# The order of a node tile's closing work in the edge loop of a graph attention layer

## The reference

```python
hh = (x @ W).reshape(n, H, D)                       # 8 heads of 32
scores = leaky_relu(s_src[src] + s_dst[dst], 0.2)
e = jnp.exp(scores - m[dst])                        # m: segment max
alpha = e / segment_sum(e, dst)[dst]
out = segment_sum(hh[src] * alpha[:, :, None], dst) + x
out = elu(layernorm(out) * gamma + beta)
x = x + out
gate_logits = layernorm(x) @ gate_w + gate_b        # then top 2 of 16 experts
```

## Time and profile before

| | us |
|---|---|
| median of three runs | 3359.18 (3358.12 to 3366.66) |
| the profiled execution, its own time | 3364.55 |
| its span in the profile | 3362.8 |

### The profile page before, as it was taken

One profiled execution on the slowest core, in us unless ns is written; L12 is line 12 of the kernel. 1 busy time (PEld: TensorE's weight loads), 2 busy tenths in 40 slices (PEclk: granted clock), 3 DMA queues, 4 the chain that ended last, 5 costly groups with the idle time before them and its releaser, 6 DMA issues. The chain is left out here.

```text
span 3362.8 us, 43456 instructions
## 1 busy us (share of the span) xinstructions
PE 1790.6 (53%) x9190; PEld 1462.5 (43%) x9191; DVE 1683.8 (50%) x3940; ACT 1018.8 (30%) x2031; POOL 1840.0 (55%) x1936
## 2 busy tenths in 40 slices
PE   6243544445454454544535444454544535999975
PEld 5132433334343343433434333343433435898964
DVE  6554545545455464554645445454554542333346
ACT  4232323233232332323233232332323312333442
POOL 2455656566565666656566565665656523555520
PEclk9676777777677776777767777776777767999987
DMA  5443434434343343433434344343443436333343
GB/s 185 114 116 98 122 103 125 116 106 119 105 123 116 107 119 105 123 110 115 117 105 123 102 125 117 107 119 103 124 118 106 119 82 205 101 103 101 106 142 130
DMA packets 184424, 393.55 MB, mean 117 GB/s; under 512 B 52129, under 2 KB 106810, under 8 KB 178116
## 3 DMA queue, kind: packets, MB, share of 16 engines
q0 software_dynamic: 92288, 267.12, 27.9%
q1 hardware_dynamic: 75876, 111.73, 10.7%
q10 hardware_dynamic: 16224, 14.30, 1.5%
HBM read 356.52 MB, written 36.47 MB: 117 GB/s over the span
## 5 line engine op out<-in xcount | busy, mean ns | idle before, releaser
L1265 POOL DMA_INDIRECT gat<-table,idx x1632 | 1547.0, 948 | 999.0 <-issue 452.5
L1362 PE MATMUL ps_sum<-msg,hot 128*128 128x264 f32 x3332 | 1076.1, 493 | 1049.3 <-DVE msg L1409 779.1
L1362 PEld LDWEIGHTS ps_sum<-msg,hot 128*128 128x128 f32 x3332 | 815.2, 250 | 1252.2 <-issue 1067.0
L1409 DVE TENSOR_TENSOR msg<-gat,ps_weight 128x2304 f32<-128x2304 f32 x196 | 473.5, 2416 | 399.9 <-ACT ps_weight L1321 391.0
L1560 DVE TENSOR_TENSOR num<-acc,ps_sum 128x264 f32<-128x264 f32 x49 | 21.0, 430 | 692.4 <-remote 681.5
L1277 ACT ACTIVATE hotT<-dst_row,neg_id 128x4352 bf16<-128x4352 int16 x48 | 188.3, 3922 | 285.3 <-remote 271.8
L1679 ACT ACTIVATE std<-var 128x1 f32<-128x1 f32 x49 | 9.9, 203 | 832.7 <-DVE var L1571 824.1
L1406 DVE TENSOR_TENSOR hot<-ps_own,rel 128x1152 f32<-128x1152 f32 x196 | 251.0, 1281 | 0.0
L1348 PE MATMUL ps_look<-dst_split,hotT 128*128 (+1 forms) x1666 | 80.9, 191 | 280.5 <-ACT hotT L1279 266.0
L2089 PE MATMUL ps_ht<-xT,w_t 128*128 128x128 f32 x1712 | 215.0, 280 | 2.0 <-DVE w_t L2122 1.6
L2089 PEld LDWEIGHTS ps_ht<-xT,w_t 128*128 128x128 f32 x1712 | 202.9, 194 | 6.9 <-DVE w_t L2122 4.6
(11 more groups left out here) (395 smaller groups left out, 2049.7 us busy)
## 6 DMA issues: line engine op xcount, KB each, us to landing
dst_row<-dst_half SPq DMA_DIRECT2D x49, 1088.0 KB
gat<-table,idx POOLq DMA_INDIRECT x1666
b_t<-in_L_ffn_b_dram ACTq DMA_DIRECT2D x107, 128.0 KB
w_sb<-in_L_ffn_w_dram SPq DMA_DIRECT2D x6, 2048.0 KB, 12.5
listing<-list_f SPq DMA_DIRECT2D x736, 0.5 KB
back<-chosen SPq DMA_DIRECT2D x5, 1792.0 KB, 10.0
table<-rows SPq DMA_DIRECT2D x49, 128.0 KB, 1.7
y_rows<-y SPq DMA_DIRECT2D x49, 128.0 KB
```

The lines of the kernel that those rows point to most:

```text
L1265: pool.indirect_dma_start(gat[:, GSTART[g] + k, :], None, table, bass.IndirectOffsetOnAxis(ap=idx[g][:, k:k + 1], axis=0)).then_inc(landed ...
L1362: last = pe.matmul(ps_sum[:, 0:SUM], hot[:, m, k, :], msg[:, m, k, :], start=(g == 0 and k == 0), stop=(g == NG - 1 and k == n - 1))
L1409: dve.tensor_tensor(msg[:, m, 0:n, 0:D].rearrange("p j (h d) -> p j h d", d=HD), gat[:, j:j + n, 0:D].rearrange("p j (h d) -> p j h d", d=HD),
```

## The change

VectorE's list for a tile no longer begins with `sums` of the last tile. It does group 0 of the new tile first, then `scale_outer` of tile t-2, then `sums` of tile t-1. `scale_inner` moves from behind group 0 to behind group 1, `lift` from group 1 to group 2, `join` from group 2 to group 3, where it stands ahead of `hand_over` of tile t-2. On ScalarE `root_inner` moves from ahead of group 0 to ahead of group 1, with a table load for the exponential behind it; `root_outer` stays ahead of group 0 with its own load; `centre` moves from group 1 to group 2 and `lower` from group 2 to group 3. The lists of TensorE, POOL and SyncE stay as they are.

```diff
--- before.py
+++ after.py
@@ -1298,18 +1298,20 @@
                     cast(t + 1)
                 if old >= 1:
                     finish.norm_inner(act, t - 1)
-                    finish.root_inner(act, t - 1)
-                    if old >= 2:
-                        finish.root_outer(act, t - 2)
+                if old >= 2:
+                    finish.root_outer(act, t - 2)
                     act.preload_act_table(ACT.Exp)
                 for g in range(NG):
                     m, n = g % 2, GROUPS[g]
                     if g == 1 and old >= 1:
-                        finish.centre(act, t - 1)
+                        finish.root_inner(act, t - 1)
+                        act.preload_act_table(ACT.Exp)
                     if g == 1 and old >= 2:
                         finish.norm_outer(act, t - 2)
                         finish.turned(act, t - 2, ps_t)
                     if g == 2 and old >= 1:
+                        finish.centre(act, t - 1)
+                    if g == NG - 1 and old >= 1:
                         finish.lower(act, t - 1)
                     if g == 2 and old >= 2:
                         finish.odds(act, t - 2)
@@ -1412,22 +1414,22 @@
                                   ALU.mult).then_inc(msg_ready, 1)
 
             def tile(t, head, old, last=False):
-                if old >= 1:
-                    finish.sums(dve, link, t - 1, ps_sum)
                 for g in range(NG):
                     group(t, g, head)
-                    if g == 0 and old >= 1:
-                        finish.scale_inner(dve, link, t - 1)
                     if g == 0 and old >= 2:
                         finish.scale_outer(dve, link, t - 2)
+                    if g == 0 and old >= 1:
+                        finish.sums(dve, link, t - 1, ps_sum)
                     if g == 1 and old >= 1:
-                        finish.lift(dve, link, t - 1)
+                        finish.scale_inner(dve, link, t - 1)
                     if g == 1 and old >= 2:
                         finish.choose(dve, link, t - 2, ps_route)
                     if g == 2 and old >= 1:
-                        finish.join(dve, link, t - 1)
+                        finish.lift(dve, link, t - 1)
                     if g == 2 and old >= 2:
                         finish.place(dve, link, t - 2, ps_route, iota)
+                    if g == NG - 1 and old >= 1:
+                        finish.join(dve, link, t - 1)
                     if g == NG - 1 and old >= 2:
                         finish.hand_over(dve, t - 2, ps_route)
```

## The result

The changed kernel takes 3569.36 us (median of four runs, 3523.53 to 3582.28) where the kernel before takes 3362.92 us beside it (four runs, 3358.12 to 3367.52): a ratio of 1.057, with an interval of 1.053 to 1.061. That is slower. The forecast was 3295 us, faster; 3569 us lies above the range as well.

What follows compares the result with a forecast made beforehand. Waits, not work, were taken to bind: VectorE to POOL at a tile's head, POOL's gather runs after. 52.9 less 51.5 is 1.4 us a tile, 64 us over 46 tiles: 3295 us, range 3215 to 3515.

Steps and rivals of the forecast that it cites:

- the loop's own second: SyncE: the loop's own time between the last listing and dst_row, put at 1 us.
- Step (5): SyncE's listings, then dst_row at S+29.4 (S: tile's last sum_done seen); group 3's msg at S+45.2, tile ends S+51.5.
- step (2): POOL: 3.39 us stop for group 0's msg goes, stop for its sum is 2.5 us; cycle saves 2.4 to 2.6 us.
- the stop at S+11: POOL: after a run of 8 gathers ending at S+10.8, a 2.5 us stop for group 0's sum.
- Step (1): VectorE: group 0's 5.1 us move into the 14.2 us idle before sums; its sum starts at S+0.7, not S+8.1.
- step (3): VectorE: join ahead of hand_over makes list_ready 2.1 us later; all still done before S, against 14.3 us at present.
- Steps (3) and (4): VectorE and ScalarE: steps moved one group on, one more Sqrt and Exp load, 1.28 us each; loads cost nothing, uncovered 2.6.
- Rival A: SyncE: listings not done before the run of 17 gathers is deep; one short gives 56.2 us, 3511 us; chance 0.37.
- the threshold S+31: SyncE: with dst_row later than S+31, group 3's msg ends the tile later than today.
- the margin of 1.6 us: SyncE: the listing count's spare time before dst_row passes S+31, less than half of one listing deep in a run.
- B: SyncE isn't held by gather runs as counted, POOL's full gain: 50.3 us a tile, 3239 us; chance 0.15.
- C: POOL: the saved 3.4 us return as waits for group 0's sum and group 3's msg; 52.8 us, 3355 us; chance 0.10.

Runs made afterwards that it cites:

- e5: The changed kernel without an edit, measured again in a series where the kernel before takes about 2860 us: 2859.81 us, ratio 1.000 to the kernel before.
- h2: The changed kernel with TensorE giving each sum_done only once POOL has come to its wait for it: 3346.83 us, ratio 0.995 to the kernel before.
- s1: The kernel before with each listing's address loaded twice on SyncE: 3475.48 us, ratio 1.033 to the kernel before.
- s2: The changed kernel with each listing's address loaded twice on SyncE: 4044.32 us, ratio 1.204 to the kernel before.
- g2: The changed kernel with sums back at the head of VectorE's tile, the other moved steps and table loads kept: 3359.21 us, ratio 0.999 to the kernel before.
- e2: The kernel before with the next tile's dst_row issued ahead of the 16 listings: 2857.32 us, ratio 0.999 to the kernel before.
- k2: The kernel before with dst_row ahead of the 16 listings, in a slow-signal series: 3397.38 us, ratio 1.002 to the kernel before.

## Why the prediction was wrong, point by point

The forecast was a tile of 51.5 us; it took 58.1. The difference of 6.6 us has three terms, by the means over all tiles. (The forecast's own terms for the row, 26, 2.2 and 1, add up to S+29.2; it went on with S+29.4, and so does this table.)

| step | forecast | measured | difference |
|---|---|---|---|
| last listing issued | S+28.4 | S+29.4 | +1.0 |
| from it to dst_row ("the loop's own second") | 1.0 | 5.2 | +4.2 |
| landing, to hotT | 5.5 | 5.45 | 0 |
| hotT to the next S (7.75 + 2.5 + 6.3) | 16.6 | 18.1 | +1.5 |

**Step (5), SyncE.** Here the time was lost, mostly as a consequence of step (2) below. The count of listings came out nearly right, by two errors that cancel: 4 and not 3 of the 16 were out at S, and the stop at S+11, in and behind which 3.6 more were to get out, didn't exist in 31 of 42 tiles. What was mis-sized is the piece behind them. Between the last listing and `dst_row` SyncE does its loop's branch, an address load and a wait that is long fulfilled. That takes 1.78 us on the mean in the kernel before and 1.72 in e5, and I put it at 1. In the changed kernel it takes 2.4 in the 8 tiles that have the stop, and 5.8 in the 31 that don't: there the last listing goes at S+30.2, deep in the run of 9 gathers that begins at S+24 (5.2 over all tiles). The trace shows single instructions of SyncE there (line 1228, the address of the row; durations in ns), in the tile above, and under it the same line's assertion over the loop in e5:

```profile
L1228 SPq TENSOR_LOAD <-lo_i x1: 679/679/679, 1561.0 to 1561.0; - x1
L1228 SPq FUSED_REGOPS  x1: 699/699/699, 1561.7 to 1561.7; - x1
L1228 SPq SEQ_ASSERT  x1: 703/703/703, 1562.4 to 1562.4; - x1
```

```profile
L1228 SPq SEQ_ASSERT  x81: 18/18/23, 462.5 to 2171.5; - x81
```

An assertion, which issues no DMA and takes 18 ns in e5, takes 703 here. Of the nine instructions between the last listing and the row's issue in this tile, five last about 0.7 us, and three start 0.7 us after the one before has ended. So it isn't SyncE's DMAs alone that are held; its other instructions are too. The price deep in a run is one per instruction, and not one per listing as I counted it. The prediction weighed the Trainium skill, DMA: Bandwidth & Descriptors, SWDGE vs HWDGE vs iDMA, by which the queues are served in turn inside a DMA engine. The runs don't speak against that rule: the row landed in 5.45 us. It bears on the transfer, and the time was lost ahead of it.

**Step (2), POOL's stop for group 0's sum.** This is the step that failed, and its value fed step (5). I took 2.5 us between the bounds 0.3 and 3.8. In 31 of 42 tiles there was no stop: in the tile shown POOL's queue was past its wait by S+7.6 (1535.97), before its engine had come to it, and ran on to 17 gathers. In the 8 tiles that have the stop it measured 2.5 us, and `dst_row` went at S+29.2, both as forecast; h2, which forces the stop, has the row at S+28.9. So the missing stop is worth 6.8 us of the row's place, 36.0 less 29.2. I had seen that sums whose records begin within a run are told of late, and applied it as a stop; I hadn't asked what follows when the sum starts at S+0.6 and is told of in time. The last part of the prediction names this failure: "group 0's sum told of at S+8 (then a run of 17 from S on and SyncE held longer)". Yet it had no chance of its own.

**Step (1), group 0 ahead.** TensorE took up group 0's sum at S+0.6 (forecast S+0.7). But its cover was priced in a tile in which VectorE idles 14.2 us ahead of `sums`. When msg of group 3 ends the tile, that idle time is gone: behind it stand `join` and `hand_over` (2.3 us) and group 0 (5.1 us), 7.4 us against TensorE's own 6.46 us for the sum. For a cover of 6 us the prediction weighed the 5.1 alone; where it added `join` and `hand_over`, in step (3), it held them against the present 14.3. s1 and s2 measure the whole of it: 16.42 and 18.09 us from `hotT` to S, 1.7 us for the new order.

**Steps (3) and (4).** Hidden in the old order, as forecast: g2, which has nothing else of the change, gives 0.999. In the new order `join`'s place is part of the 1.7 us above.

**The decision point.** Rival A had the mechanism, and the threshold S+31. With the measured pieces it is 52.9 less 5.45 less 18.08, S+29.4: exactly the place at which the forecast put `dst_row`. So the margin of 1.6 us that carried the choice between the forecast and A was nothing; even with the row where I had it, the tile would have taken what it took before. The 8 tiles with the stop show just that: 53.0 us. A's price for one listing short, 56.2 us, is under the 58.1 measured. Of the others, B wanted 50.3 us a tile and 3239 us; with the row first the change reaches 51.2 us and 3279 us. That is close to my forecast of 51.5 us, which the change as made never reached. C didn't happen in these conditions.

## What to carry to other kernels

Before a queue's list is left as it is because its result "has long landed", work out how late it may get, and price every instruction of that list, the loop's branch and address loads too, at what they cost in the stretch in which they will now fall. A cover is to be checked in the tile as it will be, with the new last step, and not in the tile of before. And where a small DMA on which the next tile depends stands behind a batch on which nothing depends soon, it goes ahead of the batch: that one edit turned a loss of 5.7% into a gain of 2.5%, in the slow-signal series; in the others neither order is worth anything.

## What the runs showed of the hardware

The same program takes two times. The kernel before took 2851 to 2860 us in series e, f and m, and 3362 to 3391 us in the others and in the first measurement. It doesn't go by the number of the chip alone: chip number 5 had 2851 us in series f and 3364 in series g. Nearly all of the difference lies in the edge loop, where long runs of indirect gathers are issued: for one kernel, in e2 and k2, 535 of 539 us come before the last closing sum. In the slow kind two things are late during such a run, and a gather is as long as ever (948 against 950 ns): SyncE's instructions, as shown above, and TensorE's signals. A long run alone doesn't do it: in e2 and e5 no gap between two gathers is over 0.32 us from 440 to 2200 us, and neither is late there. The latter show in the wait of VectorE for the closing sum, the same kernel (row first, before) in a series of each kind, e2 and then k2:

```profile
L1565 DVE TENSOR_TENSOR num<-acc,ps_sum 128x264 f32<-128x264 f32 x42 | 18.0, 429 | 254.0 <-PE ps_sum L1367 254.0
```

```profile
L1565 DVE TENSOR_TENSOR num<-acc,ps_sum 128x264 f32<-128x264 f32 x40 | 17.1, 428 | 576.9 <-remote 576.9
```

6.0 us a tile against 14.4. Register instructions on VectorE, ScalarE and GpSimd are not stretched: none of theirs in the changed kernel's loop is over 0.6 us, against 12 to 26% of SyncE's, by kind. The traces differ in one more thing: e5's holds 45,006 semaphore events and the changed kernel's first one 20,782 for the same program. The Trainium skill, NOTIFIC — the notification-queue block, Interfaces, says that backpressure from the block that writes such records can stall an engine; no run here shows that this is what happens. What is backed up, and whether it belongs to the chip, its neighbours or the recording of the profile, stays open.
